# The causal mask of the maximum pass: from matmuls of TensorE to the maximum instruction of VectorE

## What is computed

```python
scores = jnp.einsum('bhqd,bhkd->bhqk', q, k) * SCALE
causal = jnp.tril(jnp.ones((s, s), dtype=bool))
scores = jnp.where(causal, scores, -jnp.inf)
weights = jax.nn.softmax(scores, axis=-1)
out = jnp.einsum('bhqk,bhkd->bhqd', weights, v)
```

## Time and profile before

| what | value |
|---|---|
| median of three runs | 2214.8 us (2208.49 to 2218.28) |
| the profiled execution, its own time | 2213.8 us |
| its span, first to last instruction | 2211.8 us |
| mean granted TensorE clock | 0.974 |
| TensorE matmul busy | 2042.2 us, 92%, 15696 instructions |
| VectorE busy | 1844.0 us, 83%, 3611 instructions |
| ScalarE busy | 1343.4 us, 61%, 1637 instructions |
| GpSimd busy | 252.1 us, 11% |
| DMA | 178.25 MB, mean 81 GB/s |

### The profile page before, as it was taken

One profiled execution on the slowest core, in us unless ns is written; L12 is line 12 of the kernel. 1 busy time (PEld: TensorE's weight loads), 2 busy tenths in 40 slices (PEclk: granted clock), 3 DMA queues, 4 the chain that ended last, 5 costly groups with the idle time before them and its releaser, 6 DMA issues.

```text
span 2211.8 us, 39573 instructions
## 1 busy us (share of the span) xinstructions
PE 2042.2 (92%) x15696; PEld 850.2 (38%) x15696; DVE 1844.0 (83%) x3611; ACT 1343.4 (61%) x1637; POOL 252.1 (11%) x349
## 2 busy tenths in 40 slices
PE   6997699999999999999999999999999997799997
PEld 3664123333333333333333333333333323566664
DVE  6885798989998988889898898989898963899983
ACT  3664166677777677777767667767766674233332
POOL 4000011100101011010101110010101102322000
PEclk9999599999999999999999999999999998999999
DMA  3999800313214040421403041231404004554320
GB/s 109 284 282 236 177 11 15 83 38 67 63 35 93 7 92 21 85 50 48 90 11 92 18 80 38 66 68 33 92 6 93 12 22 125 139 138 114 92 70 30
DMA packets 169098, 178.25 MB, mean 81 GB/s; under 512 B 20178, under 2 KB 143314, under 8 KB 168914
## 3 DMA queue, kind: packets, MB, share of 16 engines
q1 hardware_dynamic: 162002, 163.12, 29.9%
q0 software_dynamic: 6912, 12.61, 2.6%
HBM read 107.76 MB, written 67.63 MB: 79 GB/s over the span
## 4 chain that ended last, share of the span: by engine, by line
PE 56%; DVE 21%; ACT 7%; issue 3%; SPq 1%; DMA 1%; POOL 0%; ACTq 0%; DVEq 0%; POOLq 0%
PE b_psO L942 20%; PE b_psS L924 15%; DVE b_pmax L820 13%; PE b_ring L896 12%; ACT b_prob L861 5%; PE c_psH L1294 3%; PE b_ring L893 3%; PE c_psO L1307 2%; PE c_psA L1264 1%; DVE c_attn L103 1%; DVE c_ln_x_stats L79 1%; DVE c_ln_f_stats L79 1%; DVE c_x L1137 1%; DVE c_ffn L1185 1%; DVE c_y L103 1%
## 5 line engine op out<-in xcount | busy, mean ns | idle before, releaser
L820 DVE TENSOR_REDUCE b_pmax<-b_ring 128x1 f32<-128x512 f32 (+4 forms) x2336 | 1377.2, 647 | 178.2 <-PE b_ring L896 172.9
L861 ACT ACTIVATE b_prob<-b_psS 128x1024 f32<-128x1024 f32 (+3 forms) x1280 | 1082.7, 896 | 455.5 <-PE b_psS L924 451.1
L924 PE MATMUL b_psS<-g_qT,g_kT 64*128 64x512 bf16 (+7 forms) x5120 | 752.0, 347 | 19.4 <-ACT b_prob L861 12.8
L896 PE MATMUL b_ring<-g_kT,g_qT 64*128 64x512 bf16 (+3 forms) x2560 | 700.0, 354 | 12.1 <-DVE b_pmax L820 7.7
L942 PE MATMUL b_psO<-b_prob,g_v 128*32 128x512 f32 (+3 forms) x5120 | 601.0, 542 | 1.2 <-POOL b_prob L806 0.3
L924 PEld LDWEIGHTS b_psS<-g_qT,g_kT 64*128 64x128 bf16 (+1 forms) x5120 | 289.1, 94 | 217.0 <-ACT b_prob L861 92.3
L896 PEld LDWEIGHTS b_ring<-g_kT,g_qT 64*128 64x128 bf16 x2560 | 201.1, 95 | 437.6 <-DVE b_pmax L820 362.0
L806 POOL TENSOR_SCALAR_AFFINE_SELECT b_prob<-b_prob 128x512 f32<-128x512 f32 x256 | 163.1, 637 | 1660.0 <-ACT b_prob L861 1660.0
L893 PE MATMUL b_ring<-later,query_of 64*128 64x128 bf16 x1024 | 179.6, 225 | 49.0 <-PEq L284 33.2
L893 PEld LDWEIGHTS b_ring<-later,query_of 64*128 64x128 bf16 x1024 | 79.0, 94 | 257.4 <-DVE b_pmax L820 200.0
L942 PEld LDWEIGHTS b_psO<-b_prob,g_v 128*32 128x32 f32 x5120 | 101.9, 108 | 171.9 <-issue 151.5
(11 more groups left out here) (96 smaller groups left out, 1003.6 us busy)
## 6 DMA issues: line engine op xcount, KB each, us to landing
qk_parts<-a_parts SPq DMA_DIRECT2D x64, 384.0 KB, 4.5
g_qT<-qk_parts SPq DMA_DIRECT2D x192, 128.0 KB, 4.3
g_kT<-qk_parts SPq DMA_DIRECT2D x192, 128.0 KB, 4.3
v_ones<-a_v SPq DMA_DIRECT2D x64, 256.0 KB, 4.1
g_v<-v_ones SPq DMA_DIRECT2D x32, 512.0 KB, 5.8
out_sums<-b_outT SPq DMA_DIRECT2D x64, 256.0 KB, 2.9
a_x<-in_L_attn_x SPq DMA_DIRECT2D x16, 512.0 KB, 4.9
c_x<-in_L_attn_x SPq DMA_DIRECT2D x16, 512.0 KB, 7.8
```

The lines of the kernel that those rows point to most:

```text
L820: nc.vector.tensor_reduce(pmax[:, c % 2].rearrange("p (h t) n -> p h t n", t=TT)[:, heads[0]:heads[-1] + 1:2, qt, pc], ring[:, bank, 0:k * ...
L861: nc.scalar.activation(prob[:, j % PBUF, 2 * s:2 * s + 2, off:CH], psS[:, 2 * s:2 * s + 2, off:CH], ACT.Exp).then_inc(exp_done, 1)
L896: ins_ = nc.tensor.matmul(ring[:, bank, i * w:(i + 1) * w], qT[own, g, h // 2, 0, t * P:(t + 1) * P], kT[own, g, h // 2, 0, pc * CH:pc * C ...
L924: ins_ = nc.tensor.matmul(psS[:, 2 * s + p, off:CH], kT[own, g, s, ab, kt * P:(kt + 1) * P], qT[own, g, s, ab, c * CH + off:(c + 1) * CH], ...
```

## The change

The two constant tiles and their matmuls go. In their place there is one constant, mask, 128 x 512 in float32: zero, and -1e30 above the diagonal of its last 128 columns. On the diagonal VectorE adds the last w columns of it to the tile and takes the maximum in the same call, tensor_tensor_reduce, which also writes the masked tile back to the ring's bank. Each head now has a job of its own (units is gone), and the cost functions of the planner are changed to suit: the diagonal jobs cost VectorE 60 more, and TensorE half a cycle per column without the 128 of the mask.

```diff
-        self.query_of = sb("query_of", [P, P], BF16)
-        self.later = sb("later", [P, P], BF16)
+        self.mask = sb("mask", [P, CH], F32)
...
-                    for heads in units(c, qt, pc):
-                        jobs.append(["max", 0, g, c, qt, pc, heads, False])
+                    for h in range(HG):
+                        jobs.append(["max", 0, g, c, qt, pc, h, False])
...
-    return 200 if job[0] == "turn_max" else 70 + len(job[6]) * width(*job[3:6])
+    return 200 if job[0] == "turn_max" else 70 + width(*job[3:6]) + 60 * (job[5] == job[3])
...
-    return P * 4 if job[0] == "turn_max" else len(job[6]) * (width(*job[3:6]) // 2 + P * (job[5] == job[3]))
+    return P * 4 if job[0] == "turn_max" else width(*job[3:6]) // 2
...
-                    nc.vector.tensor_reduce(
-                        pmax[:, c % 2].rearrange("p (h t) n -> p h t n", t=TT)[:, heads[0]:heads[-1] + 1:2, qt, pc],
-                        ring[:, bank, 0:k * w].rearrange("p (k w) -> p k w", k=k), AX.X, ALU.max).then_inc(ring_free, 1)
+                    to = pmax[:, c % 2, h * TT + qt, pc:pc + 1]
+                    if pc == c:
+                        ins_ = nc.vector.tensor_tensor_reduce(out=ring[:, bank, 0:w], in0=ring[:, bank, 0:w],
+                                                              in1=mask[:, CH - w:CH], scale=1.0, scalar=-3.0e38,
+                                                              op0=ALU.add, op1=ALU.max, accum_out=to)
+                    else:
+                        ins_ = nc.vector.tensor_reduce(to, ring[:, bank, 0:w], AX.X, ALU.max)
+                    ins_.then_inc(ring_free, 1)
...
-                        if pc == c:
-                            nc.tensor.matmul(ring[:, bank, (i + 1) * w - P:(i + 1) * w],
-                                             query_of[half:half + HALF, :], later[half:half + HALF, :],
-                                             start=True, stop=False, skip_group_check=True)
...
-                                                start=pc < c, stop=True, skip_group_check=pc == c)
+                    nc.tensor.matmul(ring[:, bank, 0:w], qT[own, g, h // 2, 0, t * P:(t + 1) * P],
+                                     kT[own, g, h // 2, 0, pc * CH:pc * CH + w], start=True, stop=True
+                                     ).then_inc(ring_full, 1)
```

More of the change, by code:

```diff
@@ L108 @@
 class Constants:
-    IDENT, EPS_SET, BUILT = 2, 3, 9 + E
+    IDENT, EPS_SET, BUILT = 2, 3, 5 + E
     LOADS = 4
@@ L139, in build_rest @@
     def build_rest(self, pool):
[L143 to L163, removed]
+        self.nc.gpsimd.memset(self.mask[:, :], 0.0).then_inc(self.set, 1)
+        pool.wait_ge(self.set, 4)
+        diagonal = self.mask[:, CH - P:CH]
+        self.nc.gpsimd.affine_select(out=diagonal, in_=diagonal, compare_op=ALU.is_ge, fill=NEG, base=0,
+                                     pattern=[[-1, P]], channel_multiplier=1).then_inc(self.set, 1)
         for e in range(E):
-            pool.wait_ge(self.set, at + e)
+            pool.wait_ge(self.set, 5 + e)
             self.nc.gpsimd.memset(self.place[:, e:e + 1], float(e - E)).then_inc(self.set, 1)
@@ L566 @@
 SWITCH = 500
[L569 to L575, removed]
 def max_jobs():
@@ L688 @@
 N_BODY = sum(len(slot) for slots in BODY_JOBS for slot in slots)
-assert N_BODY % BANKS == 0 and BK % PBUF == 0
+assert BK % PBUF == 0
 def stage_b(nc, consts, groups, chunks):
@@ L701, in sem @@
             return ctx.enter_context(nc.semaphore(name))
-        ident, query_of, later = consts.ident, consts.query_of, consts.later
+        ident, mask = consts.ident, consts.mask
         qT, kT, vS, loaded = groups.qT, groups.kT, groups.vS, groups.loaded
@@ L815, in do @@
                 if job[0] == "max":
-                    _, q, g, c, qt, pc, heads, ends = job
-                    k = len(heads)
+                    _, q, g, c, qt, pc, h, ends = job
                     w = width(c, qt, pc)
                     v.wait_ge(ring_full, r + 1)
-                    nc.vector.tensor_reduce(
-                        pmax[:, c % 2].rearrange("p (h t) n -> p h t n", t=TT)[:, heads[0]:heads[-1] + 1:2, qt, pc],
-                        ring[:, bank, 0:k * w].rearrange("p (k w) -> p k w", k=k), AX.X, ALU.max).then_inc(ring_free, 1)
+                    to = pmax[:, c % 2, h * TT + qt, pc:pc + 1]
[6 more added lines that the diff above has]
+                    ins_.then_inc(ring_free, 1)
                     if ends:
@@ L842, in body @@
                     for job in sum(slots, []):
-                        do(job, it * N_BODY + i, i % BANKS, it)
+                        do(job, it * N_BODY + i, (it * N_BODY + i) % BANKS, it)
                         i += 1
@@ L882, in do @@
                 if job[0] == "max":
-                    _, q, g, c, qt, pc, heads, ends = job
+                    _, q, g, c, qt, pc, h, ends = job
                     t = TT * c + qt
                     w = width(c, qt, pc)
-                    if c == qt == pc == heads[0] == 0:
+                    if c == qt == pc == h == 0:
                         pe.wait_ge(loaded[g], (it + q + 1) * 16 * LOADS)
-                    half = heads[0] % 2 * HALF
+                    half = h % 2 * HALF
                     own = slice(half, half + KA)
-                    for i, h in enumerate(heads):
-                        if pc == c:
-                            nc.tensor.matmul(ring[:, bank, (i + 1) * w - P:(i + 1) * w],
-                                             query_of[half:half + HALF, :], later[half:half + HALF, :],
-                                             start=True, stop=False, skip_group_check=True)
-                        ins_ = nc.tensor.matmul(ring[:, bank, i * w:(i + 1) * w],
-                                                qT[own, g, h // 2, 0, t * P:(t + 1) * P],
-                                                kT[own, g, h // 2, 0, pc * CH:pc * CH + w],
-                                                start=pc < c, stop=True, skip_group_check=pc == c)
-                    ins_.then_inc(ring_full, 1)
-                    return heads[0] % 2
+                    nc.tensor.matmul(ring[:, bank, 0:w], qT[own, g, h // 2, 0, t * P:(t + 1) * P],
+                                     kT[own, g, h // 2, 0, pc * CH:pc * CH + w], start=True, stop=True
+                                     ).then_inc(ring_full, 1)
+                    return h % 2
                 else:
@@ L947, in body @@
                         for job in slots[s]:
-                            behind = do(job, it * N_BODY + i, i % BANKS, it)
+                            behind = do(job, it * N_BODY + i, (it * N_BODY + i) % BANKS, it)
                             i += 1
```

## The result

The changed kernel takes 2249.2 us (median of four runs, 2245.3 to 2251.7) where the kernel before takes 2216.4 beside it: a ratio of 1.0157, 95% interval 1.0138 to 1.0177. It is slower by 33 us, as forecast, but by less than the 56 us of the forecast. The profiled execution took 2245.3 us with a span of 2243.4, at a mean clock of 0.972.

What follows compares the result with a forecast made beforehand. TensorE and VectorE were taken to bound the kernel together. VectorE's stage work, 1399 + 20 + 123 = 1542 us, made a pass 203.7 us against 196.8: 2213.8 + 56 = 2270 us, range 2215 to 2380.

Steps and rivals of the forecast that it cites:

- VectorE's pair extra: On VectorE in the attention stage, the second instruction behind each masked maximum adds 0.12 us, 1024 times: 123 us.
- My own point of decision: Price of VectorE's masked pair of instructions, about 0.04 us, below which less work on TensorE was to win.
- the two cancel: Rival: at a pair price of 0.04 to 0.07 us, time within 0.5% of before, about 2214 us; chance 0.12.
- The heads coming apart: On VectorE, pairs of heads split into 224 more reductions of 0.087 us fixed cost each: 20 us.
- The order as a loss: New plan puts five tiles where there were four, adding work to full steps without VectorE slack; no size of its own.
- rates of the planner: Planner's VectorE cost per TensorE cost: 0.224 before, 0.258 after, so more unmasked jobs fall to each step.
- TensorE's relief: 1024 mask matmuls leave TensorE: 55 us of the chain, seen only where TensorE leads; floor 24.0 us per stretch.
- The balance of the two engines: In full-width steps, TensorE's chain and four VectorE reductions each take 2.47 us, balanced to a hundredth.
- The signs I had named: In the profile after: short instruction at most 0.1 us, VectorE about 1540 us and above 90%, idle well below 178 us.
- Half rate: Rival: VectorE's masked maximum runs at half rate, 341 us more work, 2604 us; chance 0.05.
- the dear pair: Rival: VectorE's second instruction waits for the first to drain, costing 0.165 to 0.25 us; 2316 to 2408 us; chance 0.17.
- TensorE was the bound: Rival: second instruction hidden, VectorE grows by 20 us only, TensorE's 55 us return in good part: 2182 us; chance 0.08.

Runs made afterwards that it cites:

- the first experiment: Each head's diagonal tile in a bank and reduction of its own, mask still by matmuls, old cost functions, against the kernel before: 2256.4 us, 1.0204.

## Why the prediction was right, and where it was not

Add up the change along the experiments, in the order of before: heads into two banks +2.66%, mask from TensorE to VectorE +0.24%, new plan -1.33%; together 1.57%. (By another path the parts come out a little otherwise: with the masks on VectorE the two banks are 2.1%.) The sign was right, and the time lies in the range. But of the terms that gave 56 us most were wrong in size and one in sign, and they made up for one another: that the sum came near was in good part luck.

- **VectorE's pair extra, 0.12 us.** Mis-sized: 0.03 us from start to start at 512 columns, and 44.4 us / 1024 = 0.04 by the busy time with and without the masks. It lay within my bounds of 0 to 0.25, but I took the middle between two rows of other kinds. The lower bound's reason, that the short instruction hides behind the long one, was the true one. VectorE's work in the stage became 1460 us, not 1542.
- **My own point of decision.** At 0.04 us the working gave about 2205 and "the two cancel"; the kernel took 2249 (profiled 2245). So the whole of the loss, and some 10 us more, came from somewhere that the working did not have. With the right price I would have forecast no change, and been wrong.
- **The heads coming apart, 20 us of work.** This is the step that failed. As work it is 20.3 us in two banks and 11.9 in one, where it is hidden (1.0003); the fixed 0.087 us for each reduction were too much there, 11.9 / 224 = 0.053. But two narrow heads in one bank are also twice the depth of a ring of three. I had written that three tiles stand in a row "as many as there are banks" and never asked what the ring held before: in the order of before it costs 59 us.
- **The order as a loss.** Five tiles in full steps did put runs of five reductions on the chain. (The rows of three full tiles, 14 and 99 in the order of the instructions, are 44 and 99 in the planner's lists, where no mask matmul parts them.) But the new plan gains 1.33% (29 us) over the order of before, with the mask on VectorE in both, and 0.77% over the first experiment's with the mask on TensorE. Why it gains was not taken apart. The prediction's rates of the planner are also miscounted: the cost functions of the two kernels give 161304 / 406104 = 0.397 and 170944 / 389720 = 0.439, a growth of 10% and not of 15. The jobs of a pass, 300 and 328, are right, and the sum uses no rate.
- **TensorE's relief.** The floor of 24.0 us gave back half of the mask time of a stretch, 8.1 x 8 x 0.65 = 42 us in all if TensorE set every stretch. Measured: 1.05% (23 us) in the kernel before, 0.55 to 0.66% apart. A share of the chain, 55 us, was no estimate of what leaves with it.
- **The balance of the two engines.** This held. TensorE's matmuls gone and VectorE's instructions added are nearly a trade: the same move costs 0.24, 0.30, 0.76 and 0.90% in four pairs of kernels of one order and banks each, and is in none of them a gain. The first two are within the noise, and no run has a plan of its own for shared banks with VectorE's masks.
- **The signs I had named.** The first instruction lasts 0.720 us at 512 columns, not 0.68; the short one's own time is hidden, and so below 0.1. Busy 1460 us and 90%, not 1540 and above 90. Idle time before the ring's tiles fell from 178.2 to 111.3 + 44.5 = 155.8 us, not well below. The chain of VectorE is 27%, not half. The time outside the stage and the clock stayed, small dips aside.
- **The rivals.** Half rate and the dear pair fall by the timeline. "TensorE was the bound" falls in part: its relief is real, 23 us in the kernel before, but with VectorE's masks in the same order and banks the sum is a loss of 0.79%.

## What to carry to other kernels

Where a ring of few slots joins two engines, count what a slot holds in the consumer's time, not only the work: a slot with one small tile where there were two covers half as much of the producer's next long job, and here that cost 59 us where the work added was 20. Read the price of a new instruction from start to start, and when a forecast has several parts, run them one at a time in the old order: here the parts were +59, +5 and -29 us, and the smallest was the one that the change was about. Before a mask is moved to another engine, ask whether the value needs it at all.

## What the runs showed of the hardware

*The read of the accumulator is hidden.* It is a record of 140 ns, 1024 times, 143.4 us, and starts together with the next masked instruction. From start to start the pair takes 0.65 us at 512 columns where the plain reduction takes 0.618. The Trainium skill (Vector Engine (DVE) Microarchitecture Reference, section 5.2) states about 75 ns per instruction for its one- and two-source operations; a read has no source, and behind its own instruction the trace shows about half of that.

*The masked instruction runs at full rate.* The plain reductions of the kernel with one bank and two reductions, by form, to be held against the masked ones above:

```profile
L821 DVE TENSOR_REDUCE b_pmax<-b_ring 128x1 f32<-128x512 f32 x1792 | 1131.2, 682 | 131.3 <-PE b_ring L897 126.7
L821 DVE TENSOR_REDUCE b_pmax<-b_ring 128x1 f32<-128x384 f32 x256 | 126.5, 548 | 13.7 <-PE b_ring L897 13.7
L821 DVE TENSOR_REDUCE b_pmax<-b_ring 128x1 f32<-128x256 f32 x256 | 91.0, 415 | 16.0 <-PE b_ring L897 15.9
L821 DVE TENSOR_REDUCE b_pmax<-b_ring 128x1 f32<-128x128 f32 x256 | 57.9, 282 | 11.1 <-PE b_ring L897 10.8
```

720, 587, 451 and 311 ns against 682, 548, 415 and 282: 0.03 to 0.04 us more at every width, so next to nothing per column, with one input in PSUM, one in SBUF and the output back in PSUM.

*Instructions of VectorE overlap.* Reductions that last 0.683 us start 0.618 us apart. The Trainium skill (VectorE: DVE Perf Modes, section "The DRAIN you can't avoid") says that the next instruction does not start until the pipe has emptied, and adds that one which nothing holds starts earlier; the addition fits, since by the records the next one starts 0.065 us before the end of the one ahead.
